# Prologue and first unit of a transformer block: a head restacked in halves, rows and items in another order, remainders of the weights spread over units 0 to 3

## The reference

```
emb = t @ w + b;  scale, shift = split(emb)             # adaptive norm, three of them
h1 = layernorm(x) * (1 + scale) + shift
q, k, v = h1 @ wq, h1 @ wk, h1 @ wv                     # 256 -> 1024 each, 16 heads of 64
x = softmax(q @ k.T / 8) @ v @ wo + bo + x              # then the same over the context
x = (a * gelu(gate)) @ w2 + b2 + x                      # then the ternary layer
```

## Time and profile before

| | us |
|---|---|
| median of 3 runs (lowest, highest) | 1165.55 (1163.76, 1167.77) |
| the profiled execution | 1171.97, span 1169.9 |
| TensorE busy in the span | 1076.2 (92%) |
| VectorE, ScalarE, POOL busy | 817.3, 613.0, 698.8 |
| mean granted clock of TensorE | 0.972 of 2.4 GHz |

### The profile page before, as it was taken

One profiled execution on the slowest core, in us unless ns is written; L12 is line 12 of the kernel. 1 busy time (PEld: TensorE's weight loads), 2 busy tenths in 40 slices (PEclk: granted clock), 3 DMA queues, 4 the chain that ended last, 5 costly groups with the idle time before them and its releaser, 6 DMA issues.

```text
span 1169.9 us, 30528 instructions
## 1 busy us (share of the span) xinstructions
PE 1076.2 (92%) x12740; PEld 683.8 (58%) x12740; DVE 817.3 (70%) x1365; ACT 613.0 (52%) x1112; POOL 698.8 (60%) x641
## 2 busy tenths in 40 slices
PE   4688999999999999999999999889899989999995
PEld 1235556556656656656656556567677766756663
DVE  6556677567566567678676576858778866787887
ACT  3344555554554554555554555544445444258678
POOL 5655877775666667778676667436535633533433
PEclk7688999999999999999999999999999989999999
DMA  8240202211201202202202203213534253000001
GB/s 293 55 126 2 56 2 56 56 24 34 56 16 42 56 13 45 56 2 56 56 2 56 56 2 91 66 32 77 139 64 89 60 131 127 1 1 10 14 15 37
DMA packets 35197, 63.51 MB, mean 54 GB/s; under 512 B 10947, under 2 KB 21871, under 8 KB 32757
## 3 DMA queue, kind: packets, MB, share of 16 engines
q1 hardware_dynamic: 33757, 60.90, 20.6%
q10 hardware_dynamic: 1304, 0.66, 0.2%
HBM read 20.63 MB, written 2.10 MB: 19 GB/s over the span
## 4 chain that ended last, share of the span: by engine, by line
PE 66%; DVE 18%; DMA 5%; ACT 5%; issue 4%; POOL 2%; SPq 0%; ACTq 0%; DVEq 0%; POOLq 0%
PE outs L794 9%; PE scores L859 8%; DVE neg_max L1797 7%; PE scores L860 7%; PE outs L771 6%; PE scores L920 5%; DMA head_operands<-neg_max_rows 4%; PE outs L881 4%; PE outs L934 4%; PE outs L883 4%; PE outs L882 3%; PE outs L804 3%; PE mixed L816 2%; PE scores L794 2%; PE outs L833 2%
## 5 line engine op out<-in xcount | busy, mean ns | idle before, releaser
L1527 POOL TENSOR_TENSOR exps_rest<-exps 128x1024 f16<-128x1024 f32 (+1 forms) x297 | 512.2, 1730 | 284.9 <-ACT exps L1201 284.2
L1201 ACT ACTIVATE exps<-scores 128x512 f32<-128x512 f32 (+1 forms) x576 | 328.4, 595 | 281.4 <-PE scores L860 262.4
L881 PE MATMUL outs<-values,exps 128*128 128x65 f16 (+1 forms) x2176 | 229.0, 193 | 3.2 <-DVE attn_out L1825 2.0
L859 PE MATMUL scores<-head_operands 128*128 128x512 f16 (+1 forms) x576 | 220.8, 383 | 9.6 <-DMA head_operands<-neg_max_rows 7.1
L882 PE MATMUL outs<-values,exps 128*128 128x64 f16 (+1 forms) x2176 | 228.8, 193 | 0.0
L883 PE MATMUL outs<-values,exps_rest 128*128 128x65 f16 (+1 forms) x2176 | 228.4, 195 | 0.0
L881 PEld LDWEIGHTS outs<-values,exps 128*128 128x128 bf16 (+1 forms) x2176 | 202.5, 99 | 38.6 <-issue 12.4
L860 PE MATMUL scores<-head_operands 128*128 128x512 f16 (+1 forms) x576 | 219.8, 382 | 0.0
L882 PEld LDWEIGHTS outs<-values,exps 128*128 128x128 bf16 (+1 forms) x2176 | 201.9, 98 | 22.1
L883 PEld LDWEIGHTS outs<-values,exps_rest 128*128 128x128 f16 (+1 forms) x2176 | 201.8, 97 | 0.0
L1797 DVE TENSOR_REDUCE neg_max<-mixed 128x1 f32<-128x1024 f32 x128 | 156.2, 1220 | 42.5 <-PE mixed L817 41.3
(11 more groups left out here) (209 smaller groups left out, 1796.6 us busy)
## 6 DMA issues: line engine op xcount, KB each, us to landing
head_operands<-qk_pairs SPq DMA_DIRECT2D x64, 256.0 KB, 3.1
head_operands<-qk_pairs SPq DMA_DIRECT2D x32, 512.0 KB, 5.5
head_operands<-qk_pairs SPq DMA_DIRECT2D x32, 128.0 KB, 2.3
stage<-in_L_xcond_ff_w_dram SPq DMA_DIRECT2D x3, 1024.0 KB, 5.6
residual<-in_x_dram SPq DMA_DIRECT2D x4, 512.0 KB, 9.8
stage<-in_L_ffn_w_dram SPq DMA_DIRECT2D x2, 1024.0 KB, 5.0
head_operands<-in_x_dram SPq DMA_DIRECT2D x1, 2048.0 KB, 9.2
out_dram<-head_operands SPq DMA_DIRECT2D x16, 128.0 KB, 1.7
```

What stands on the lines that cost most here:

```text
L859: mm(o, kb[:, KH, :], hb[:, QS, :], start=True, stop=False)
L881: mm(o, eb[:, sl], vb[:, DH:VW], start=(kt == 0 and q == 0), stop=False, skip_group_check=True)
L1201: A(E[0:a.ks, c % RING, j * HALF:(j + 1) * HALF], score_bank(a, c, j), ACT.Exp, scale=SCALE).then_inc(s.exps, 1)
L1527: G.tensor_tensor(R[0:a.ks, c % RING, 0:n], e, e.bitcast(BF16).rearrange("p (n two) -> p n two", two=2)[:, :, 1], ALU.subtract).then_inc(s ...
```

## The change

The second and later units keep their list, the prologue and FIRST_UNIT are new.

- The prologue splits only the 128 weight columns (per half) that unit 0 needs (`first_pair`); the other 1792 columns of q, k and v, the *rest*, are split in unit 0 (`split`, `scaled`, with `rest_low` on POOL for q and v and `keys_low` on VectorE for k). Wo is split in unit 1, its low part in four pieces by VectorE in unit 2 (before: POOL, unit 1).
- ScalarE normalises the first 8 tiles straight from x into the operand (`first_scale` on POOL makes scale and shift columns with one power); the residual itself gets its own pass later (`tokens_x`, units 1 and 2), and the bias addition (`rows_x`) moves to units 2 and 3. There are four h_full buffers for these tiles. The statistics of tokens 8 to 11 move into unit 0, those of 12 to 15 into unit 1.
- The norm's columns are made directly: conditioning as the moving operand (2 columns), the weights as the stationary one, biases transposed once.
- q 1 is made after k 1 and behind the first maxima. Head 0 of unit 0 takes its maxima from ST, unstacked, by two products on the same 64 rows. Head 0 is restacked in two halves of 512 columns, the first as soon as q 0 and k 0 are there.
- The first row (`first`) is transposed ahead of v 0 and v 1, and the scores wait for the first half (and chunk 2 for the second).
- The context's transposes stand behind the second maximum, the later norms' columns (`embed`) within unit 0.

The core of the diff; the order lists, renamed semaphores and counts are left out:

```diff
 FIRST_UNIT = (
-    ("max", 0, 0, 0), ("max", 0, 0, 1), ("max", 0, 0, 2), ("max", 0, 0, 3), ("setup", "rows"), ("v", 0, 0),
-    ("first", 0, 0), ("max", 0, 0, 4), ("max", 0, 0, 5), ("v", 0, 1), ("setup", "columns"), ("scores", 0),
...
+    ("split", 0), ("max", 0, 0, 0), ("max", 0, 0, 1), ("setup", "columns"), ("scaled", 0), ("max", 0, 0, 2),
+    ("max", 0, 0, 3), ("q", 0, 1), ("rest", 0), ("first", 0, 0), ("max", 0, 0, 4), ("max", 0, 0, 5), ("v", 0, 0),
+    ("v", 0, 1), ("scores", 0), ("max", 0, 0, 6), ("max", 0, 0, 7), ("scores", 1), ("q", 1, 0), ("scores", 2),
+    ("split", 1), ("rest", 1), ("row", 0, 0), ("scores", 3), ("rest", 2), ("split", 2), ("setup", "embed"),
+    ("scores", 4), ("max", 0, 1, 0), ("max", 0, 1, 1), ("scores", 5), ("q", 1, 1), ("values", 0), ("scaled", 2),
+    ("scores", 6), ("rest", 3), ("scores", 7), ("k", 1, 0), ("values", 1), ("setup", "tokens"), ("max", 0, 1, 2),
...
@@ notes @@
+        if (g, c) == (1, 10):
+            self.add("setup", what="stats12")
+        if (g, c) == (1, 5):
+            self.add("split", c=3)
+        if g == 2 and c in (3, 6, 9, 12):
+            self.add("split_low", what=c // 3 - 1, c=3)
+        if g in (1, 2) and c in (3, 6, 9, 12):
+            self.add("tokens_x", c=4 * g - 5 + c // 3)
+        if g in (2, 3) and c in (2, 7, 10, 14):
+            self.add("rows_x", c=4 * g - 8 + (2, 7, 10, 14).index(c))
@@ attention @@
+            if t >= 2:
+                self.norm("hi", t - 2)
+                self.norm("lo", t - 2)
+            if t in (1, 3, 5):
+                self.add("first_pair", c=t // 2)
+            if t == TPB - 1:
                 first_item("q", 0, 2)
+        first_item("k", 0, 4)
+        first_item("k", 1, 7)
+        self.add("setup", what="ones")
@@ restack @@
+                if (ai, g) == (0, 0):
+                    hb = HB[:, 0, 0, :, :]
+                    for i, done in enumerate((first_half, s.heads[0])):
+                        c = slice(i * HALF, (i + 1) * HALF)
+                        sp.wait_ge(s.qk, 2 + 2 * i)
+                        sp.dma_start(hb[0:DH, QS:KH + 1:KH - QS, c], ST[0:DH, Q_HI:K_HI + 1, c]).then_inc(done, 16)
+                        sp.dma_start(hb[DH:P, :, c], ST[0:DH, :, c]).then_inc(done, 16)
@@ TensorE @@
             def embed(i):
-                for k in range(KC):
-                    last = mm(embedded[i], condT[:, k, :], nw[:, i, k, :], start=(k == 0), stop=(k == KC - 1))
+                for c in range(4):
+                    for k in range(KC):
+                        last = mm(PV_[1][:, (4 * i + c) * B:(4 * i + c + 1) * B], nw[:, i, k, c * P:(c + 1) * P],
+                                  condT[:, k, :], start=(k == 0), stop=(k == KC - 1))
...
+                    if (ai, g, h) == (0, 0, 0):
+                        if t % TPH == 0:
+                            pe.wait_ge(s.qk_hi, 3 + t // TPH)
...
+                        for i in range(2):
+                            last = mm(m[:, i * HALF:(i + 1) * HALF], ST[0:DH, Q_HI, t * P:(t + 1) * P],
+                                      ST[0:DH, K_HI, i * HALF:(i + 1) * HALF], start=True, stop=True)
...
                 if (ai, g, c) == (0, 0, 0):
                     pe.wait_ge(first_loaded, 16)
+                    pe.wait_ge(cleared, 16)
+                    pe.wait_ge(first_half, 32)
+                elif (ai, g, c) == (0, 0, 2):
+                    pe.wait_ge(s.heads[0], 16 * a.restack_dmas + CREDIT)
@@ ScalarE @@
+            def first_tokens(t):
+                act.wait_ge(x_shift, t // 4 + 1)
+                act.wait_ge(nrm_done, t + 1)
+                A(xr[:, t, :], xr[:, t, :], ACT.Identity, scale=xrs[:, 0, t:t + 1],
+                  bias=xnorm[:, 3, t:t + 1]).then_inc(ln1_first, 1)
+            def pair_hi_part(n):
+                act.wait_ge(w_loaded[n], 16)
+                A(first_pair(W[:, n, 0, :]), first_pair(raw[:, n, :]), ACT.Copy, scale=WS).then_inc(pair_hi, 1)
...
+                    if (ai, g, what) == (0, 1, ("q", 0)):
+                        act.wait_ge(s.maxed, TPB)
@@ POOL @@
+            def first_scale(g):
+                G.tensor_scalar(xtmp[:, 0, c], xmv[:, c, 1], 1.0 + EPS, EPS * EPS, ALU.mult, ALU.add).then_inc(x_prod, 1)
+                G.tensor_tensor(xnorm[:, 2, c], xmv[:, c, 0], mi, ALU.mult).then_inc(x_prod, 1)
+                G.tensor_tensor(xnorm[:, 0, c], xtmp[:, 0, c], mh, ALU.pow).then_inc(x_scale, 1)
+                G.tensor_tensor(xnorm[:, 1, c], xnorm[:, 2, c], xnorm[:, 0, c], ALU.mult).then_inc(x_cols, 1)
+            def rest_low(n):
+                pool.wait_ge(w_scaled, 1 + n // 2)
+                lo, src, hi = rest_of(W[:, n, 1, :]), rest_of(raw[:, n, :]), rest_of(W[:, n, 0, :])
+                G.tensor_tensor(lo, src, hi, ALU.subtract).then_inc(rest_done[n], 1)
@@ VectorE @@
+            def keys_low():
+                dve.wait_ge(split_hi, 2)
+                V.scalar_tensor_tensor(out=rest_of(W[:, 1, 1, :]), in0=rest_of(raw[:, 1, :]), scalar=WS,
+                                       in1=rest_of(W[:, 1, 0, :]), op0=ALU.mult, op1=ALU.subtract).then_inc(rest_done[1], 1)
```

324 lines of the change are left out of this document (180 added, 144 removed).

## The result

| | before | after |
|---|---|---|
| median of 6 runs each (lowest, highest), us | 1169.33 (1163.76, 1175.48) | 1155.93 (1155.22, 1159.44) |
| the profiled execution; its span | 1171.97; 1169.9 | 1157.49; 1155.7 |
| a second profile of each; its span | 1169.19; 1167.2 | 1154.48; 1152.7 |
| mean granted clock as the view gives it, first and second profile | 0.972, 0.982 | 0.985, 0.988 |

The ratio of the times is 0.9894, interval 0.9864 to 0.9924: faster by 1.1%, 12 us by the ratio and 13 by the medians, where 25 were forecast. Before's own time scatters by 12 us from run to run, after's by 4.

What follows compares the result with a forecast made beforehand. TensorE was taken to bound the kernel from 162.3 us on, earlier stretches only delaying it. Gains of 20.8 + 5.8 - 1.5 = 25.1 us from 1165.55 gave 1140.5, range 1134 to 1147 (ends of all terms 1129 to 1155).

Steps and rivals of the forecast that it cites:

- First scores: Stretch ahead of unit 0's scores: they start at 38.5 instead of 59.3, 20.8 us earlier (18.1 to 24.0).
- The columns' products: Prologue, norm columns: 8 products with 2 moving columns, costing between nothing and 2.2 us, off the path.
- the v weights' landing: Prologue: ScalarE's third weight step waits for the v weights until 15.3; tile 7 is transposed by 17.7.
- a sign of error: Prologue: the forecast was to be wrong if tiles 6 and 7 don't wait for the v weights.
- the cold walk: Prologue chain at the lower clock: q 0 and k 0 from 17.7 to 22.9, first maximum at 26.1, end at 41.2.
- my cold and warm walks: Prologue chain at the lower and the upper clock level, ending at 41.2 and 35.3; 38.5 was taken between them.
- Unit 0: First unit of the first attention: 55 us instead of 60.8, 5.8 us shorter (-3.4 to 12.9).
- The 7 us of loss: Unit 0: loss added to 47.9 us at full clock, giving 55; all of before's loss kept would give 64.2.
- Rival (a): Unit 0 takes 62 to 68 us, as added work delays exponentials and maxima; at 65, 1150.5 us; chance 0.22.
- Units 1 to 3: First attention's later units: moved passes and wo's split mostly hidden beside TensorE, 1.5 us lost (0 to 4).
- The rest of the program: Everything after unit 3: taken as unchanged, 0 us, since no line touched by the diff runs otherwise there.
- rival (c): Clock stays at the 1.2 GHz level through unit 0, making the kernel slower, 1181 us; chance 0.04.

Runs made afterwards that it cites:

- even: The changed kernel with the token pass in four slots, residual passes spread over units 2 to 5 and bias additions over units 3 to 6; ratio to before 0.9892.

## Why the prediction was wrong, step by step

**First scores, 20.8 forecast, 20.3 measured.** Right as a sum, by terms that erred both ways. The columns' products were put between nothing and 2.2 us and beside the path; they took 3.58, two instructions each at the lower clock level, ended at 12.1 instead of 10 and moved the first tile to 12. Half of them gone brought 0.8 us. The gate was not the v weights' landing (15.35, as forecast) but ScalarE's own queue: tile 7 transposed at 19.3 instead of 17.7. I had named that as a sign of error, and it is one: at that point the landing hid nothing, and that the sum still came out is luck. Against this k 0 followed q 0 at once, 5.1 us for both as in the cold walk, and k 1 ran at 2.4 GHz, 1.47 us: first maximum at 26.52 for 26.1. The clock between maximum and scores was 0.73, between my cold and warm walks. That the maxima no longer wait for a DMA is the mechanism, but the edit that undoes it costs 5 us, not the larger part.

**Unit 0, 5.8 forecast, 5.8 measured.** The 7 us of loss that I chose between nothing and all of before's are what it lost: 55.0. The products took 3.94 instead of 3, and VectorE's busy time is 43.12 for the 42.9 worked out. Rival (a) did not come about. That both terms are met to the digit is luck: in the ten profiles whose unit 0 does the changed kernel's work in its order, the first scores started anywhere from 35.7 to 40.0, the unit took 55.0 to 59.5, and the output stood at 92.8 to 95.9 without following the scores. What holds is the sum of the two terms, the output at 93.5 forecast; an earlier start was lost in a wait for VectorE's part of unit 1's q 0 (1.8 and 1.9 us against 0.6) and in more of the low clock (0.91 and 0.94 against 0.97, in the kernels with narrow additions and with wo late). The moved token steps show how little room there is: 61.2.

**Units 1 to 3, 1.5 lost (0 to 4) forecast, 6.9 and 6.4 measured.** This is the step that failed. I held that the moved passes "are hidden beside TensorE [...] as long as no exponential comes late". Three things were wrong in it. The durations: the pass over tokens 12 to 15 was left out, since before had it too, in unit 1 and in 1.38 us; in unit 2, among POOL's remainders without a pause between them, it took 4.12. Wo's pieces were taken at 0.7 and took 0.85 to 2.25. The cover: I weighed busy time against TensorE's sum, but the units' chain already ran over VectorE's maxima (2.26 us a pair) with waits of 0.7 and 0.5 left, so that whatever is put ahead of a maximum or a division shows at once. And the token steps, 18 short instructions of which 14 had been in the prologue, I counted with 1.8 us of VectorE and nothing for POOL or for the two engines' holding each other up: 2.3 us. The terms that I did price, ScalarE's passes and wo's split, left unit 1 where it was. The table above has the four steps; my range of 0 to 4 did not hold their sum.

**The rest of the program, 0 forecast.** 5.0 us longer in the first pair, 1.5 in the second. No line touched by the diff runs there, and the part varied by 4 us among kernels that are the same there. What I can show for 3.1 of the 5.0 is the low clock of the last part; the 2.1 of the second attention stay unexplained. All eighteen profiles with the change (924.9 to 928.8, mean 926.6) lie above before's two (923.7 and 924.3), so some 2 us may belong to the change after all; why stays open.

**The base.** I subtracted the 6.4 us by which the profiled execution lay above the median of three runs. With six runs before's median is 1169.33, 3.8 us higher, and later sets of 11 and 10 runs of the same kernel have medians of 1170.7 and 1172.0: the profiled execution (1171.97) was an ordinary one and the three runs were on the fast side. After's profiled execution lies only 1.6 above its own median. That is 4.8 (6.4 less 1.6) of the 15.4 us between 1140.5 and 1155.93, of which 3.8 are the median of too few runs; the other 10.6 are the profiled execution, 1157.49 for the 1146.9 forecast, and so the 5.4 of units 1 to 3 and the 5.0 of the rest. The clock plays a part in before's scatter (its rise in the prologue at 26 or only at 35 us is 3.3 us at unit 0's output), but how much of the median's distance it is was not measured. So the clearest error in reading is the units, the largest doubt is the rest.

**The rules cited.** On the shared port pair I used the rule too little. It stood in the prediction for unit 0 alone, and it shows in units 1 to 3: the four token steps took 2.7 us more than the 1.38 of before, wo's four pieces 5.5 us for the 2.8 that I reckoned, and four steps of 8 columns still 3.24. The Trainium skill (SBUF — State Buffer, "SBUF: two separate sides") says that the pair is held for a whole instruction; it limits this, which my prediction left out, to VectorE steps in a two-port mode or with two inputs in SBUF. The trace agrees: VectorE's narrow steps on SBUF data ended 0.03 us behind POOL's, and its reductions out of PSUM kept 1.21 us each beside the same work of POOL. That moving wo's low part from VectorE to POOL alone changed unit 2 by 0.2 us would fit the rule too, but the same move on top of even did change it, so this is no proof. On the clock, rival (c) did not come about: unit 0 ran at 0.97. That a sparser prologue is no warmer came out otherwise, 0.73 between first maximum and first scores where before had 0.50.

## What to carry to other kernels

Work moved out of a poor prologue into units that look 97% full is not hidden, whatever the other engines' busy shares say: follow the chain of waits within one steady unit, and look at what stands in it. Here ScalarE's passes in unit 1 were free, and those on VectorE, over whose maxima it ran, were paid in full, short ones too: a step of VectorE on SBUF data that starts beside one of POOL's passes costs what is left of POOL's instruction, whatever its own width, while its steps out of PSUM kept their time. In units 4 to 6 additions and passes of the same kind cost 0.4 us at most.

Three runs are few for a base that scatters by 12 us: the median moved by 3.8 us with three more. And where a view of the clock says 1.00, hold it against the durations of like products: here 12 of them took twice as long each as the next six, in a row with 1.00.

## What the runs showed of the hardware

- A float32 product with a 128x128 stationary operand and 2 moving columns, two instructions in the trace, took 0.45 us in the prologue (8 in 3.58), where the f16 products that follow ran at half speed, and 0.23 to 0.25 in unit 0 (16 in 3.73 and 3.94; up to 6.95 where the clock was low). Two moving columns were not cheap: a transpose with 128x128 weights took 0.27 in the same prologue.
- The same program reached the upper clock level at 26 us in one execution; in another it was at the lower one from 15.0 to 35.5 us. This was worth 2.9 us at the first maximum and 3.3 at unit 0's output.
- The same four VectorE steps took 1.38 us in a pause of POOL, 4.12 without one, and 3.24 with a 32nd of the columns; the two of the narrow ones that were held up ended 0.03 us after POOL's instruction.
